# First attention of a four-layer kernel: three-row-group operands, 1024-wide maxima, and scores, values, maxima in that order in each step

## The reference

```python
qkv = x @ Wqkv.T + bqkv
qkv = qkv.reshape(B, H, S, 3 * hd)            # H = 16, S = 2048, hd = 8
q, k, v = jnp.split(qkv, 3, axis=-1)
scores = jnp.einsum('bhsd,bhtd->bhst', q, k) * (1.0 / math.sqrt(hd))
attn = jax.nn.softmax(scores, axis=-1)
vals = jnp.einsum('bhst,bhtd->bhsd', attn, v)
vals = vals.reshape(B, S, D)
return vals @ Wo.T + bo
```

## Time and profile before

| | |
|---|---|
| time, median of 3 runs | 3474.54 us (3467.3 to 3480.65) |
| span of the profiled execution | 3463.3 us |
| PE busy | 3092.5 us (89%) |
| DVE busy | 2371.1 us (68%) |
| ACT busy | 1441.1 us (42%) |
| first attention: first max, first score, last values copied out | 75.5, 117.6, 953.3 us |

### The profile page before, as it was taken

The page is one execution under the profiler, slowest core; times in us unless marked ns, Lnnn a source line. Parts: engine busy times, 40 slices in busy tenths (PEclk is TensorE's granted clock), DMA queues, the critical chain, the costliest instruction groups (busy, mean ns, idle before and its releaser), DMA issues. The chain is left out here.

```text
span 3463.3 us, 39811 instructions
## 1 busy us (share of the span) xinstructions
PE 3092.5 (89%) x14168; PEld 1729.6 (50%) x14168; DVE 2371.1 (68%) x4742; ACT 1441.1 (42%) x2519; POOL 811.3 (23%) x623
## 2 busy tenths in 40 slices
PE   5999999999978999999999999999997575566799
PEld 3444444444354555555555555555544243444576
DVE  5877777877327777777777777777745667665553
ACT  0466666666721444444444444443442203000343
POOL 2000000000002444344444444434440000444100
PEclk6799999999986999999999999999998676555698
DMA  3011011010013111101111111111100000000100
GB/s 79 3 13 13 7 13 13 7 13 7 1 44 74 37 29 33 29 21 37 37 37 37 37 37 25 32 24 31 37 1 12 0 7 2 1 1 3 29 1 13
DMA packets 35834, 76.13 MB, mean 22 GB/s; under 512 B 5926, under 2 KB 27356, under 8 KB 28636
## 3 DMA queue, kind: packets, MB, share of 16 engines
q1 hardware_dynamic: 35636, 73.59, 10.4%
HBM read 17.74 MB, written 5.24 MB: 7 GB/s over the span
## 5 line engine op out<-in xcount | busy, mean ns | idle before, releaser
L875 ACT ACTIVATE l1a_PT<-l1a_st 128x512 f32<-128x512 f32 x1024 | 604.9, 598 | 874.8 <-PE l1a_st L784 867.8
L892 DVE TENSOR_REDUCE l1a_m<-l1a_aux 128x1 f32<-128x512 f32 x1024 | 673.4, 686 | 185.7 <-PE l1a_aux L747 170.5
L429 DVE TENSOR_REDUCE l0s_m<-l0s_mx 128x1 f32<-128x512 f32 x1024 | 634.8, 683 | 203.2 <-PE l0s_mx L351 203.2
L843 POOL TENSOR_TENSOR l1a_acc<-l1a_acc,l1a_PT 128x1024 f32<-128x1024 f32 x224 | 555.6, 2480 | 716.0 <-ACT l1a_PT L875 716.0
L414 ACT ACTIVATE l0s_PT<-l0s_st 128x512 f32<-128x512 f32 x1024 | 554.7, 601 | 325.7 <-PE l0s_st L369 320.0
L797 PE MATMUL l1a_ov<-l1a_PT,l1a_V 128*64 128x512 f32 x2048 | 510.1, 620 | 0.0
L351 PE MATMUL l0s_mx<-l0a_KS,l0a_QS 96*128 96x512 f32 x1024 | 447.2, 462 | 11.5 <-DMA l0a_KS<-qk_parts 11.5
L782 PE MATMUL l1a_st<-l1a_QA,l1a_KA 128*128 128x512 f32 x1024 | 451.2, 441 | 2.3 <-issue 2.3
L784 PE MATMUL l1a_st<-l1a_QB,l1a_KB 65*128 65x512 f32 x1024 | 413.7, 404 | 0.0
L369 PE MATMUL l0s_st<-l0a_QS,l0a_KS 97*128 97x512 f32 x1024 | 402.7, 408 | 10.9 <-ACT l0s_PT L414 8.7
L747 PE MATMUL l1a_aux<-l1a_KA,l1a_QA 128*128 128x512 f32 x1024 | 404.6, 437 | 7.1 <-DMA l1a_QA<-l1a_lo 5.5
(11 more groups left out here) (350 smaller groups left out, 3105.4 us busy)
## 6 DMA issues: line engine op xcount, KB each, us to landing
l1a_KA<-l1a_hi SPq DMA_DIRECT2D x32, 512.0 KB, 7.9
l1a_QA<-l1a_hi SPq DMA_DIRECT2D x16, 512.0 KB, 4.6
l1a_QA<-l1a_lo SPq DMA_DIRECT2D x16, 512.0 KB, 4.1
l1a_QB<-l1a_hi SPq DMA_DIRECT2D x16, 512.0 KB, 4.6
l1a_KB<-l1a_lo SPq DMA_DIRECT2D x16, 512.0 KB, 6.5
l0a_QS<-qk_parts SPq DMA_DIRECT2D x64, 64.0 KB
l0a_KS<-qk_parts SPq DMA_DIRECT2D x64, 64.0 KB
l3f_w<-in_L_ffn_w SPq DMA_DIRECT2D x3, 792.0 KB
```

Source lines behind the costliest of these rows:

```text
L429: nc.vector.tensor_reduce(m4[:, h % 2, q, c:c + 1], src, axis=AX.X, op=ALU.max).then_inc(mx_read, 1)
L843: nc.gpsimd.tensor_tensor(acc[:, h % 2, 1, :], first, PT[:, g % PT_SLOTS, :], ALU.add).then_inc(added_pool, 1)
L875: nc.scalar.activation(PT[:, g % PT_SLOTS, (u % 2) * CW:(u % 2 + 1) * CW], st[:, u % ST1, :], ACT.Exp).then_inc(exp_done, 1)
L892: nc.vector.tensor_reduce(m4[:, b, q, c:c + 1], src, axis=AX.X, op=ALU.max).then_inc(aux_read, 1)
```

## The change

`l0_project` is gone; `l0_attend` does its work too. What it does differently:

- **Operands.** `QS` and `KS` now have four groups of 24 rows (q hi, q lo, q hi against k hi, k hi, k lo), at rows 0, 32, 64 and 96, each group with a quarter of the keys (512). Row 24 of a group has the maximum against -1. A matmul uses the 24 or 25 rows of one group. 24 DMAs load a head: 12 of 64 KB for `QS`, 12 of 16 KB for `KS`.
- **Units.** A head is two units of 1024 queries, of 16 steps each, 512 steps in all. A step has two score matmuls (groups 2p, 2p+1), and one max task of two matmuls (groups 2p', 2p'+1) into one of two double banks, reduced by one DVE instruction of 1024 elements.
- **Order.** In a step: both score matmuls, in every second step the values group, then the max task, whose unit is 21 steps ahead of the scores (`LEAD0`).
- **Maxima.** They are no longer transposed: DVE joins two halves (L436), and four DMAs per unit of 128 pieces of 32 bytes put them into the four groups (L493).
- **Values.** V has 9 columns in place of 32. `ov` has one buffer in place of two, and is copied out once per unit (32 times in place of 16); the first values group of a unit waits for that copy. `ot` is four matmuls with a selection matrix.
- **Projection.** q and k are biased, scaled and rounded on ACT, chunk by chunk, and head 0 is loaded after half of the chunks are written.

```diff
+GR0 = 4
+R0 = 3 * HD0
+LEAD0 = STEPS0 + 5
+LAG0 = 3
+BUF0, MX0, ST0, PT0 = 3, 2, 3, 6
...
+    def max_step(g):
+        u, s = divmod(g, STEPS0)
+        a, b = divmod(s, 4)
+        return u, 2 * a + b % 2, b // 2
+
+    def score_step(g):
+        u, s = divmod(g, STEPS0)
+        a, b = divmod(s, 4)
+        return u, b % 2, 1 - b // 2, a
...
+                if n >= MX0:
+                    pe.wait_ge(mx_free[n % MX0], n // MX0)
...
+                    for e in range(2):
+                        r = slice(32 * (2 * pair + e), 32 * (2 * pair + e) + R0)
+                        q = QS[r, h % BUF0, half * HALF0:(half + 1) * HALF0].rearrange("r (k i) -> r i k", i=TILES0)
+                        last = nc.tensor.matmul(o[:, e, :], q[:, tile, :], KS[r, h % BUF0, :], start=True, stop=True)
...
+            def scores(g):
+                u, qc, pair, a = score_step(g)
+                h, half = divmod(u, 2)
+                if g % STEPS0 == 0:
+                    pe.wait_ge(m_placed[u % 2], 16 * GR0 * (u // 2 + 1))
+                for e in range(2):
+                    b = 2 * g + e
+                    if b >= ST0:
+                        pe.wait_ge(exp_done, b - ST0 + 1)
+                    r = slice(32 * (2 * pair + e), 32 * (2 * pair + e) + R0 + 1)
...
+            def values(k):
+                u, n = divmod(k, QUADS0)
+                pe.wait_ge(exp_done, 4 * (k + 1))
+                if n == 0:
...
+                        pe.wait_ge(o_copied, u)
...
             for key in plan[0]:
                 mx_task(key)
-            for g in range(H0 * STEPS + 5):
-                tasks = plan[g + 1]
-                some = (len(tasks) + 1) // 2
-                if g < H0 * STEPS:
-                    scores(2 * g)
-                for key in tasks[:some]:
-                    mx_task(key)
-                if g < H0 * STEPS:
-                    scores(2 * g + 1)
-                if g % 2 and LAG0 <= g < H0 * STEPS + LAG0:
-                    values((g - LAG0) // 2)
-                for key in tasks[some:]:
+            for g in range(END):
+                at = g - LEAD0
+                if 0 <= at < ALL:
+                    scores(at)
+                if at % 2 and LAG0 <= at < ALL + LAG0:
+                    values((at - LAG0) // 2)
+                for key in plan[g + 1]:
                     mx_task(key)
...
+                u, s = divmod(g, STEPS0)
+                if s == 3 and u >= 1:
+                    copy_out(u - 1)
...
+                    nc.vector.tensor_reduce(mpair[:, u % 2, tile, pair:pair + 1],
+                                            mx[:, n % MX0, :, :].rearrange("p e k -> p (e k)"),
+                                            axis=AX.X, op=ALU.max).then_inc(reduced, 1)
+                    dve.wait_ge(reduced, i + 1)
+                    dve.sem_inc(mx_free[n % MX0], 1)
...
+            def load(h):
+                sp.wait_ge(parts_out[h // TPC], 32)
+                if h >= BUF0:
+                    sp.wait_ge(st_full, 4 * STEPS0 * (h - BUF0 + 1))
...
+            place(0)
+            place(1)
+            load(0)
+            place(2)
+            place(3)
+            load(1)
+            load(2)
+            for u in range(UNITS0):
+                h, half = divmod(u, 2)
+                sp.wait_ge(m_done, u + 1)
...
+                if half == 0 and u >= 2 and h + 2 < H0:
+                    load(h + 2)
```

More of the change, by code:

```diff
@@ L221, in l0_project @@
[L221 to L283, removed]
@@ L313, in l0_attend @@
[L313 to L318, removed]
-        out = []
[L320 to L326, removed]
+    ov = ps("ov", [P, CW])
+    mx_full, mx_free = sem("mx_full"), [sem(f"mx_free{i}") for i in range(MX0)]
@@ new lines, in l0_attend, with tasks_of @@
+    rden_done = sem("rden_done")
+    ALL = UNITS0 * STEPS0
+    END = ALL + LEAD0 + LAG0 + STEPS0
+    def max_step(g):
[6 more added lines that the diff above has]
+        return u, b % 2, 1 - b // 2, a
+    def tasks_of(g):
+        out = []
+        if g < ALL:
+            out.append(("max", g))
+        if g in (2, 4, 6):
+            out.append(("v", g // 2))
+        u, s = divmod(g - LEAD0, STEPS0)
+        if s == 7 and 1 <= u <= UNITS0:
+            out.append(("ot", u - 1))
@@ L338, in mx_task @@
             def mx_task(key):
[L339 to L354, removed]
+                kind, i = key
@@ new lines, in values @@
+            def values(k):
+                u, n = divmod(k, QUADS0)
+                pe.wait_ge(exp_done, 4 * (k + 1))
+                if n == 0:
+                    if u == 0:
+                        pe.wait_ge(ov_zeroed, 1)
+                    else:
+                        pe.wait_ge(o_copied, u)
+                    if u % (2 * TPC) == 0:
+                        pe.wait_ge(v_done, u // (2 * TPC) + 1)
+                for g in (2 * k, 2 * k + 1):
+                    _, qc, pair, a = score_step(g)
+                    for e in range(2):
+                        col = 32 * (2 * qc + e)
+                        last = nc.tensor.matmul(ov[col:col + HD0 + 1, :], V[:, u // 2, KPG0 * (2 * pair + e) + a, :],
+                                                PT[:, g % PT0, e, :], start=(n == 0), stop=(n == QUADS0 - 1),
+                                                skip_group_check=True)
@@ L401, in _ @@
         def _(act):
[L402 to L409 removed]
+            act.wait_ge(b_loaded, 48)
+            nc.scalar.activation(scaled_bias[:, :], bias[:, 0:1], ACT.Copy, scale=scale).then_inc(bias_scaled, 1)
@@ L416, in _ @@
-                if n == 2 and h >= 1:
-                    copy_out(h - 1)
-            copy_out(H0 - 1)
+                for e in range(2):
+                    b = 2 * g + e
+                    act.wait_ge(st_full, b + 1)
+                    nc.scalar.activation(PT[:, g % PT0, e, :], st[:, b % ST0, :], ACT.Exp).then_inc(exp_done, 1)
+                u, s = divmod(g, STEPS0)
+                if s == 3 and u >= 1:
+                    copy_out(u - 1)
+            copy_out(UNITS0 - 1)
         @block.vector
@@ L459, in _, with place @@
-            for h in range(3):
-                load(h)
-            for h in range(H0):
-                sp.wait_ge(m_row, h + 1)
-                sp.dma_start(QS[KR0:KR0 + 1, h % 3, :, :].bitcast(F32), mrow[:, h % 2, :].bitcast(F32)
-                             ).then_inc(m_placed, 16)
-                if 1 <= h < H0 - 2:
+            def place(c):
+                at = slice(c * CW, (c + 1) * CW)
+                sp.wait_ge(rounded, c + 1)
+                sp.dma_start(parts[0, :, :, at].rearrange("i p s -> p i s"), hi[:, :, at].bitcast(F32)
+                             ).then_inc(parts_out[c], 16)
+                sp.wait_ge(split, c + 1)
+                sp.dma_start(parts[1, :, :, at].rearrange("i p s -> p i s"), lo[:, :, at].bitcast(F32)
+                             ).then_inc(parts_out[c], 16)
@@ L485, in _ @@
             sp.wait_ge(loaded.sem, loaded.all)
+        @block.gpsimd
+        def _(pool):
+            for handle in used:
+                nc.gpsimd.sem_clear(handle)
         @block.tensor
```

250 lines of the change are left out of this document (148 added, 102 removed).

## The result

| | before | after |
|---|---|---|
| median (lowest to highest), us | 3473.21 (3467.3 to 3480.65) | 3788.8 (3781.96 to 3792.45) |
| ratio, 95% interval | | 1.0912 (1.0891 to 1.0933) |
| profiled execution, span | 3463.3 | 3784.2 |
| first score, last score | 117.6, 950.7 | 88.9, 1266.2 |

A forecast was written before the change was run, and what follows sets the result against it. PE's score, exponential and values loop was taken to bound the first attention, at clock 0.5: 32 units of 35.66 us plus 5, against 837.9, less 36.6 at the start, gave +271.6 and 3746 us; range 3400 to 3860.

The forecast's parts named there:

- Clock: First attention stage: granted clock 0.5 throughout, because the change removes the gapless stretch after which it rose; chance 0.60.
- 32-row stream: Earlier sixteen fp32 records of 32 rows on two row groups: PE gapless for 10.66 us, clock 0.50; basis for forecasting 0.5.
- then stays 1.0, also in the last head where PE waits: Old kernel's attention: after rising at 118 to 123 us the clock holds 1.0, even with PE waiting.
- faster rival: First attention: clock reaches 2.4 GHz and stays, period 2.90 us, total 3421 us (3365 with no addition); chance 0.26.
- Period: Two-step attention loop at clock 0.5: 3.95 us plus 0.22 for the max pair, 4.17 us; bounds 3.95 and 4.80.
- max pair ahead of the first score: After each values group: adds two weight loads, 0.22 us, to the period; the skill's span model would give about 0.01.
- Copy of `ov`: One period per unit: values wait for the single ov buffer's copy, 1.92 us where 0.61 is counted, adding 1.3.
- `ot`, the mis-sized term: One period per unit: max task waits for its bank's reduction, small matmuls add some 0.3; +1.0 us in all.
- Start: Before the first score: loads 1 and 2 delay first maxima to near 80 us; score at 81, 36.6 earlier.
- 21 max steps (27 us): Maxima lead before the first score: said to be long done when the first maxima arrive near 80 us.
- Sum: First attention: 32 x 35.66 = 1141 us plus 5, against 837.9; less 36.6 at the start, +271.6, total 3746 us.
- the tail's 5 us: End of the first attention stage: 5 us added to the 1141 us of the 32 units.

The follow-up runs named there:

- warm_rows: Changed kernel plus 120 gapless matmuls of 24 rows, in turn on three row groups, ahead of the first score; 3806.26 us in one run.
- odd_rows: Edits of warm_full and early_copy, plus two matmuls of 24 rows instead of 128 per period in the wait ahead of the fourth score; 3744.13 us.
- warm_full: Changed kernel plus twelve gapless fp32 matmuls of 128 rows and 512 columns just ahead of the first score; 3793.62 us, ratio 1.092.
- early_copy: Changed kernel with the copy-out of ov issued on ACT one step earlier (after step 2 of a unit, not 3); 3758.14 us, ratio 1.0807.
- ot_r: Changed kernel with the four small ot matmuls in one-pass fp32r instead of four-pass fp32; 3761.37 us, ratio 1.0829.
- best_6: Changed kernel with early_copy's edit, six full-row warm matmuls, and two full-row matmuls per period, none before the first score, kept up behind the last maximum; 3419.22 us.

## Why the prediction was right

The verdict, the mechanism (a stage at half clock) and the size held, 3788.8 against 3746, in the range; two of its terms and the cause of the start did not. By its steps:

- **Clock.** 0.50 from first to last score, as forecast from the 32-row stream. `warm_rows` and `odd_rows` confirm that row. The advice of the Trainium skill ("TensorE: Matmul & The Clock Gate", "Why this matters for your kernels") to keep TensorE busy does not by itself bring the clock here: `odd_rows` has PE busy 198.5 of 200 us at 0.50. Only the runs with added matmuls on full rows had the clock come back in the loop.
- **"then stays 1.0, also in the last head where PE waits"**, which stood behind the faster rival, does not carry over. In the changed loop the clock falls even when it is up (`warm_full`). That head's scores have 97 rows and the new ones 25; but its values also have 32 columns where the new ones have 9, and the new loop has max pairs. Which of these lets the clock fall, no run tells apart. The rival was weighed at 0.26; it could not happen by the start alone.
- **Period.** 4.17 forecast, 4.14 measured, partly by errors that cancel. Score to exponential 0.94 (0.83 forecast), exponential and release 0.65 (0.66), fourth score to values 0.72 (0.61), values 1.82 (1.85): 0.18 more in sum; the max pair ahead of the first score costs 0.01 instead of 0.22. That the two sums lie 0.03 us apart is luck. On the max pair the span model of the Trainium skill ("TensorE: Matmul & The Clock Gate", Part 3, "Measured speedup vs the span model"), which I had set aside, was right: the trace has 0.01 us.
- **Copy of `ov`:** +1.3 forecast, 5.49 - 4.14 = +1.35 measured; `early_copy` takes 0.99 us of this wait away in a unit and gives 31 us.
- **`ot`, the mis-sized term:** "four small matmuls add some 0.3", +1.0 in all; measured 6.68 - 4.14 = +2.54. They are eight records with 128-column loads, 1.84 us on the path, and as they use all rows, the score no longer runs beside the max pair (0.75 more). The max bank, which the term was built on, binds nothing: DVE's reduction ends at 511.20, 0.5 us before the next max pair starts (511.72). 1.54 x 32 = 49 us, which covers the miss in the stage; `ot_r` confirms that the small matmuls are on the path, and the 0.75 us is read from the trace alone.
- **Start.** 81 forecast, 88.9 measured, and by another cause. Loads 1 and 2 were issued by 73.4 us, but the maxima of the first unit ended only at 84.7: behind the first three came three projections of V, during which DVE waited 4.7 to 5.0 us each, and I had called the "21 max steps (27 us)" "long done" without them (the timeline's first two lines).
- **Sum:** the stage took 1184.2 us where 1146 was forecast, +38: 32 x (37.04 - 35.66) = 44, less 6 for the tail's 5 us and for a first unit without copy or `ot`. With the start's +8, other stages' +3, and the median 4.6 us above the span where 11.2 was taken, -7, that is the 43 us, to rounding.

## What to carry to other kernels

A redesign onto row groups removes PE time and may cost the clock with it: here the same loop takes 4.14 us a period at 0.50 and 2.77 us at 1.00 (`warm_full`, before the clock fell). Read the granted clock of a stretch where PE does only row-group work before pricing anything, and don't take a busy PE for a fast one. If a stage must be packed so, try some full-row matmuls in a wait that exists anyway, and a shorter wait at the borders: together they gave most of the clock back here (0.97).

## What was not expected of the hardware

- PE without a gap on three row groups for 17.87 us (120 matmuls), and 198.5 us busy of 200, both at granted clock 0.50.
- With two one-pass matmuls of 128 rows and 512 columns (0.74 us) in a wait of each period, a warm start and a shorter copy wait, the scores run for 804 us (best_6) where they ran for 1177.
- At clock 0.5 a max and a score matmul on disjoint row groups started 0.01 us apart (504.97 and 504.98), their weight loads too.
